# Float32 residual by accumulating transposes, and two moved steps in an attention and convolution kernel

## The chip, the cores and the metric

The kernel runs on one core of a Trainium2 chip. A core has five engines that work side by side, each with its own queue in program order: TensorE (PE, matrix products, written to PSUM), VectorE (DVE), ScalarE (ACT), GpSimd (POOL) and SyncE (SP), which here issues all transfers. They wait for each other through semaphores only. The metric is the device time of one execution in microseconds.

## What is computed

Cut to what matters. `x` is (4, 1024, 1024) float32, `cond` (4, 1024); 16 heads of 64.

```python
scale, shift = split(cond[:, None] @ W_emb + b_emb)
xn = rms_norm(x, g_norm) * (1.0 + scale) + shift
q, k, v = heads(xn @ W_qkv)                # (b, 16, n, 64) each
q, k = rms_norm(q, g_q), rms_norm(k, g_k)
attn = softmax(q @ k.T * d ** (-0.5))
o = merge(attn @ v)
x = x + (o + o @ W_out)
y = depthwise_causal_conv1d(x, cond)       # 4 taps per channel
return x + (y + b)
```

## The kernel before, in words

**Units and pairs.** The main part is `U = 32` units, four batches of eight; a unit `u` is one pair of heads of one batch. Within a unit run eight pairs `p`, 0 to 7; each takes 128 query rows of both heads against all 1024 keys. The units are unrolled, and for each engine the order of work within a pair is written out by hand in a function `unit`. A float32 operand is carried as a high and a low float16 part, and a product is made of three float16 ones.

**The softmax chain of a pair.** `score` (L946, 12 matmuls) writes both heads' logits; DVE takes each head's maximum (L1531) and makes the bias from it (L1534); ACT takes the exponential with that bias (L1187) and the high half (L1195); DVE takes the low half (L1540). `score` of the next pair writes over the same PSUM, so it waits for both exponentials (`exp_done`). The halves are transposed by DMA and go into `attend` (L965); `inverses` (L978) are two float32 transposes of the reciprocal sums, read by ACT (L1255).

**Beside it on TensorE.** `project` (L1002) makes q, k and v of the next unit in pairs 0 to 4; `stacks` (L1014) transposes them into key and query stacks. `stacks` of the second half in pair 7 writes the keys to `misc` and then the queries to `proj[:, 0]`.

**The output.** From unit 8 on (`outs`), a unit also makes output block `T = u - 8`, 512 channels (on the partitions, 128 at a time) of 256 positions, in four products `out_product(T, par, hh, i)`, one for each 128 channels: 24 float16 matmuls with `W_out` (L1036), then two float32 matmuls that add the transposed block of x (L1042). The identity operand `eye_x` of these holds the factor `back = 1 / y_scale`, since PSUM holds the output in another scale; DVE sets the two scales of the batch in `y_now` (`set_scale`) and ACT scales the identity (`scaled_eye`), every second unit. Products (0,0) and (0,1) go to bank `proj[:, 0]`, (1,0) and (1,1) to `proj[:, 1]`. `read_y(T, hh)` on ACT (L1286) copies one bank to `yT`, times `y_scale`; `convolve` on DVE (L1673 to L1684) makes the taps of a quarter of it; `out_transposes` (L1054, four float32 transposes) and `read_out` (L1299) turn it back, and SP stores it.

**Where they stood.** On TensorE, products (0,0) and (0,1) in pair 5, (1,0) in pair 6, (1,1) in pair 7. `read_y(T, .., 0)` on ACT stood at the head of pair 6, `read_y(T, .., 1)` in pair 0 of the next unit. The query stacks of pair 7 wait for `y_ev` of that first read, as they write over its bank:

```python
stacks(w, 1, 1, misc[:], (h_ev, 3 * w + 1))
stacks(w, 1, 0, proj[:, 0, :], (y_ev, 2 * T + 1) if outs else ...
```

**The end.** Unit 31 has no next unit; block 23 is made in its pairs 0 to 3, and 24 begun in pairs 4 to 7 (`tail_begin`, and `add_x`, L1023, for its residual). The blocks 25 to 31 follow one after another (`tail_product`), with their x in nine buffers `last_xr` that SP fills late. A product of block T there is followed by transposes of block T-1 or T-2. POOL's list has the powers (L1447), low halves (L1452, L1461, L1472, L1476) and nothing of the output.

## Time and profile before

| | us |
|---|---|
| median of 3 runs | 2456.92 (2450.82 to 2458.89) |
| the profiled execution, its own time | 2456.85 |
| its span, first to last instruction | 2454.9 |
| TensorE (PE) busy | 2337.2, 95% |
| DVE busy | 2061.2, 84% |
| ACT busy | 1797.1, 73% |
| POOL busy | 648.6, 26% |
| L1036, products with W_out, 3072 matmuls | 273 ns each |
| L1042 and L1023, residual, 512 records | 275 ns each |
| granted TensorE clock, mean | 0.992 |

How to read it: a matmul's length in the records includes a pipeline that overlaps the next one; what one costs in a stream is the distance from start to start. A float32 matmul stands in the trace as two records, a float32 transpose as one. TensorE being busy for 95% doesn't tell by itself whether it sets the end, since another engine may finish each step at the same moment; for that one needs the order of time around the waits.

### The profile page before, as it was taken

The numbers are of one execution on the slowest core, as the hardware profiler recorded it, in microseconds if no ns is written. First come the engines' busy times: TensorE is split into PE (matmuls) and PEld (weight loads), VectorE is DVE, ScalarE is ACT, GpSimd is POOL, SyncE is SP. The second block draws the span as 40 slices with busy tenths as digits, with TensorE's granted clock in tenths as the row PEclk, the third lists the DMA queues.
The fourth block names the chain that finished last, engine by engine and source line by source line (L and its number), as shares of the span: only waits on it lengthen the run. The fifth ranks groups of instructions, "written<-read, shape, count | busy, mean of one in ns | idle before, by whom it ended". The sixth has DMA issues, their size and how long they took to land.

```text
span 2454.9 us, 53605 instructions
## 1 busy us (share of the span) xinstructions
PE 2337.2 (95%) x20666; PEld 1529.3 (62%) x20666; DVE 2061.2 (84%) x3239; ACT 1797.1 (73%) x2706; POOL 648.6 (26%) x451
## 2 busy tenths in 40 slices
PE   5799898988899999999999999999999999999899
PEld 0455555555466666666666666666666666666688
DVE  7768988888878898888888888888888888888876
ACT  5467788788777777777777787777777777777732
POOL 1122333333333222323322223233212222222100
PEclk9899999999999999999999999999999999999999
DMA  8989989899999999999999999999988998889971
GB/s 361 315 208 230 194 177 200 180 189 225 202 207 181 203 183 215 182 200 231 204 208 191 213 183 201 192 189 222 208 177 172 182 175 162 177 162 176 186 187 52
DMA packets 1234732, 484.94 MB, mean 198 GB/s; under 512 B 1139632, under 2 KB 1197872, under 8 KB 1232048
## 3 DMA queue, kind: packets, MB, share of 16 engines
q1 hardware_dynamic: 1234480, 481.53, 93.4%
q8 instruction: 164, 2.69, 0.5%
q14 instruction: 88, 0.72, 0.1%
HBM read 137.20 MB, written 56.66 MB: 79 GB/s over the span
## 4 chain that ended last, share of the span: by engine, by line
PE 72%; DVE 11%; SPq 4%; issue 3%; ACT 2%; DMA 2%; POOL 1%; ACTq 0%; POOLq 0%
PE proj L1002 32%; PE proj L1036 12%; PE scores L946 11%; PE values L965 11%; DVE p_pair L1540 4%; DVE neg L1531 4%; SPq L750 3%; PE proj L1042 2%; PE values L978 1%; ACT p_pair L1195 1%; DMA w_sb<-w_dram 1%; PE misc L1054 1%; PE misc L1014 1%; PE proj L1014 1%; SPq L706 1%
## 5 line engine op out<-in xcount | busy, mean ns | idle before, releaser
L1002 PE MATMUL proj<-w_sb,xn_sb 128*128 128x384 f16 x6144 | 1034.1, 327 | 26.4 <-DMA w_sb<-w_dram 18.2
L1002 PEld LDWEIGHTS proj<-w_sb,xn_sb 128*128 128x128 f16 x6144 | 592.8, 98 | 431.3 <-issue 50.4
L1187 ACT ACTIVATE late<-scores,bias,l_scale 128x1024 f32<-128x1024 f32 x512 | 615.9, 1204 | 332.6 <-DVE bias L1534 313.7
L1540 DVE TENSOR_TENSOR p_pair<-late,p_pair 128x1024 f16<-128x1024 f32 x512 | 616.4, 1245 | 173.5 <-ACT p_pair L1195 173.2
L1531 DVE TENSOR_REDUCE neg<-scores 128x1 f32<-128x1024 f32 x512 | 623.2, 1217 | 101.7 <-PE scores L946 98.7
L1195 ACT ACTIVATE p_pair<-late 128x1024 f16<-128x1024 f32 x512 | 510.0, 1046 | 0.0
L965 PE MATMUL values<-pT,v_pair 128*64 128x256 f16 x6144 | 385.3, 275 | 13.2 <-ACT inv_all L1255 13.2
L946 PE MATMUL scores<-late 64*128 64x512 f16 x3072 | 376.1, 378 | 18.1 <-ACT late L1187 17.6
L965 PEld LDWEIGHTS values<-pT,v_pair 128*64 128x64 f16 x6144 | 316.4, 110 | 91.8 <-issue 70.1
L1447 POOL TENSOR_TENSOR rs<-ms,power 128x16 f32<-128x16 f32 x63 | 183.1, 2906 | 400.2 <-DVE ms L1554 399.9
L1036 PE MATMUL proj<-late,wo 128*128 128x256 f16 x2304 | 267.5, 273 | 0.8 <-DMA late<-in_x 0.8
L1476 POOL TENSOR_TENSOR oT_pair<-oT,oT_pair 128x256 f16<-128x256 f32 x124 | 148.4, 1197 | 436.2 <-ACT oT_pair L1264 436.2
L946 PEld LDWEIGHTS scores<-late 64*128 64x128 f16 x3072 | 128.9, 94 | 197.8 <-issue 45.0
L1036 PEld LDWEIGHTS proj<-late,wo 128*128 128x128 f16 x2304 | 222.3, 98 | 30.4 <-issue 5.8
L1452 POOL TENSOR_TENSOR qk_pair<-stage,qk_pair 128x512 f16<-128x512 f32 x126 | 147.1, 1189 | 327.2 <-ACT qk_pair L1218 327.2
L1684 DVE SCALAR_TENSOR_TENSOR late<-late,taps 128x256 f32<-128x256 f32 x324 | 157.1, 485 | 11.6
L1255 ACT ACTIVATE inv_all<-values 128x256 f32<-128x256 f32 x128 | 48.9, 382 | 139.0 <-PE values L978 138.9
L1203 ACT ACTIVATE stage<-proj 128x384 f32<-128x384 f32 x256 | 123.0, 480 | 25.4 <-PE proj L1002 25.4
L1534 DVE TENSOR_SCALAR bias<-neg,l_scale 128x1 f32<-128x1 f32 x512 | 109.6, 214 | 18.1
L1472 POOL TENSOR_TENSOR pair<-x_in,pair 128x1024 f16<-128x1024 f32 x24 | 66.9, 2788 | 207.2 <-ACT pair L1249 199.7
L1187 ACT ACTIVATION_READ_ACCUMULATOR late<-scores,bias,l_scale 128x1 f32 x512 | 98.6, 193 | 0.0
L1036 PE MATMUL proj<-xn_sb,wo 128*128 128x256 f16 x744 | 86.5, 273 | 0.8 <-ACT late L1286 0.8
(178 smaller groups left out, 1939.2 us busy)
## 6 DMA issues: line engine op xcount, KB each, us to landing
w_sb<-w_dram SPq DMA_DIRECT2D x121, 384.0 KB, 4.1
o_dram<-oT_pair SPq DMA_DIRECT2D x124, 128.0 KB, 2.4
out<-late SPq DMA_DIRECT2D x54, 256.0 KB, 2.9
x_in<-in_x SPq DMA_DIRECT2D x25, 512.0 KB, 4.8
late<-in_x SPq DMA_DIRECT2D x25, 512.0 KB, 4.2
wq_raw<-in_L_cond_W_qkv SPq DMA_DIRECT2D x8, 1536.0 KB, 10.7
late<-o_dram SPq DMA_DIRECT2D x12, 1024.0 KB, 6.3
xn_dram<-late SPq DMA_DIRECT2D x21, 512.0 KB, 3.3
```

Of the source, the lines that this page charges most:

```text
L946: last = nc.tensor.matmul(scores[:, h, n * HN:(n + 1) * HN], stack[rows_, par, i, p * P:(p + 1) * P], stack[rows_, par, j, n * HN:(n + 1) ...
L965: last = nc.tensor.matmul(values[DH * h:DH * h + DH, 0:QG].rearrange("p (a n) -> p a n", a=2), v_pair[:, par, 2 * c + h, DH * i:DH * i + D ...
L1002: last = nc.tensor.matmul(proj[:, t % 2, 0:6 * DH], xn_sb[:, t, i * K + c, :], w_sb[:, c, j, :], start=(c == 0 and i == j == 0), stop=(c = ...
L1036: last = nc.tensor.matmul(dst, const["wo"][:, c, b, m * P:(m + 1) * P], oT_[:, c, a, :], start=(c == 0 and a == b == 0 and c1 == K), stop= ...
L1187: nc.scalar.activation(prob[:, h, :], scores[:, h, :], ACT.Exp, bias=bias[:, s:s + 1], scale=const["l_scale"][:, 0:1], accum_out=total[:, ...
L1195: nc.scalar.activation(p_pair[:, s % 4, 0, :], prob[:, h, :], ACT.Copy).then_inc(hi_done, 1)
L1447: nc.gpsimd.tensor_tensor(rs[:], ms[:], const["power"][:, 0:4 * KH], ALU.pow).then_inc(h_pw, 1)
L1452: last = nc.gpsimd.tensor_tensor(qk_pair[:, j, 1].rearrange("p t (h d) -> p (t h) d", d=DH), stage[:, hf, :, j * DH:(j + 1) * DH], qk_pair ...
L1476: nc.gpsimd.tensor_tensor(o_half(u, g, 1), oT[:], o_half(u, g, 0), ALU.subtract).then_inc(o_low, 1)
L1531: nc.vector.tensor_reduce(neg[:, s:s + 1], scores[:, h, :], axis=AX.X, op=ALU.max, negate=True).then_inc(max_done, 1)
L1540: nc.vector.tensor_tensor(p_pair[:, s % 4, 1, :], prob[:, h, :], p_pair[:, s % 4, 0, :], ALU.subtract).then_inc(lo_done, 1)
L1684: nc.vector.scalar_tensor_tensor(out=acc_[:, m, :], in0=y_[:, m, k:k + QG], scalar=const["taps"][:, k, c:c + 1], in1=acc_[:, m, :], op0=AL ...
```

## The change

The residual's two float32 matmuls of a product become two float32 transposes against the plain identity that accumulate onto the product in PSUM. The factor `back` goes into x itself: a new POOL operation `x_residual(T)` multiplies the loaded block (128x1024 float32) in place, in pair 3 of a unit, in pairs 0, 2 and 4 of unit 31, and behind it for the rest. TensorE waits for its semaphore `xr_up` where it waited for the load and the scaled identity. `eye_x`, `one`, `y_now`, `set_scale` and `scaled_eye` are gone; `read_y` takes its scale from `const["y_scale"]`. The second product of a unit moves from pair 5 to pair 6, the first read of the output on ACT from pair 6 to pair 7. The diff, without tiles, semaphores and calls that only lose an argument:

```diff
@@ -1016,13 +1012,12 @@
                 last.then_inc(h_tr, 1)
 
             def add_x(hh, xr_):
-                pe.wait_ge(last_xr_ld[1], 16)
-                pe.wait_ge(eye_done, U - K + 2)
+                pe.wait_ge(xr_up, U - K + 1)
                 for i in range(2):
                     for a in range(2):
                         nc.tensor.matmul(proj[:, hh, i * QG + a * P:i * QG + (a + 1) * P],
-                                         xr_[:, a, (2 * hh + i) * P:(2 * hh + i + 1) * P], eye_x[:],
-                                         start=False, stop=False)
+                                         xr_[:, a, (2 * hh + i) * P:(2 * hh + i + 1) * P], const["eye32"][:],
+                                         start=False, stop=False, is_transpose=True)
 
             def out_product(T, par, hh, i, oT_, xr_, free, c0=0, c1=K):
                 m = 4 * par + 2 * hh + i
@@ -1040,7 +1035,7 @@
                     return
                 for a in range(2 if c0 == 0 else 0):
                     last = nc.tensor.matmul(dst[:, a * P:(a + 1) * P], xr_[:, a, (2 * hh + i) * P:(2 * hh + i + 1) * P],
-                                            eye_x[:], start=False, stop=(a == 1))
+                                            const["eye32"][:], start=False, stop=(a == 1), is_transpose=True)
                 if i == 1:
                     last.then_inc(op_mm, 1)
                 elif T == U - 1 and hh == 1:
@@ -1068,8 +1063,7 @@
 
             def tail_product(i, hh, c0=0):
                 T, g = U - K + i, i // 2
-                free = ((last_oT_ld[g], 16), (o_low, NG * (U - 1) + g + 1), (last_xr_ld[i + 1], 16),
-                        (eye_done, U - K + 2), (y_ev, 2 * T + hh - 1))
+                free = ((last_oT_ld[g], 16), (o_low, NG * (U - 1) + g + 1), (xr_up, T + 1), (y_ev, 2 * T + hh - 1))
                 for m in range(2):
                     out_product(T, i % 2, hh, m, last_oT[g], last_xr[i + 1], free if m == 0 else (), c0)
 
@@ -1111,18 +1105,20 @@
                     if outs and p >= 5 and not last:
                         if T == 0 and p == 5:
                             pe.wait_ge(wo_lo, K)
-                        free0 = ((oT_ld, 8 * (T - par) + 16), (xr_ld, 16 * (T + 1)), (eye_done, T - par + 2),
+                        free0 = ((oT_ld, 8 * (T - par) + 16), (xr_up, T + 1),
                                  (qkv_ev, K * w + 7) if qkv else (y_ev, 2 * T - 1))
                         free1 = ((h_ev, 3 * w + 2) if qkv else (y_ev, 2 * T),)
                         if p == 5:
                             out_product(T, par, 0, 0, oT_in, xr, free0)
+                        elif p == 6:
                             out_product(T, par, 0, 1, oT_in, xr, ())
+                            out_product(T, par, 1, 0, oT_in, xr, free1)
                         else:
-                            out_product(T, par, 1, p - 6, oT_in, xr, free1)
+                            out_product(T, par, 1, 1, oT_in, xr, ())
                     if last and p < 4:
                         hh = p // 2
                         out_product(T, par, hh, p % 2, oT_in, last_xr[0],
-                                    ((oT_ld, 8 * (T - par) + 16), (last_xr_ld[0], 16), (eye_done, T - par + 2),
+                                    ((oT_ld, 8 * (T - par) + 16), (xr_up, T + 1),
                                      (y_ev, 2 * T) if hh else (h_ev, 3 * U)))
                     elif last:
                         tail_begin((p - 4) // 2, p % 2)
@@ -1269,14 +1265,7 @@
                 nc.scalar.activation(const["wo"][:, c, 0, :], wo_raw[c], ACT.Copy,
                                      scale=wo_top[:, 3:4]).then_inc(wo_hi, 1)
 
-            def scaled_eye(T):
-                act.wait_ge(y_set, T + 2)
-                need(act, op_mm, 2 * T)
-                nc.scalar.activation(eye_x[:], const["eye32"][:], ACT.Copy,
-                                     scale=y_now[:, 1:2]).then_inc(eye_done, 2)
-
-            def read_y(T, scales, hh):
-                act.wait_ge(y_set, scales)
+            def read_y(T, hh):
                 act.wait_ge(op_mm, 2 * T + hh + 1)
                 if T == U - K - 1:
                     act.wait_ge(h_lo, 2 * U)
@@ -1285,14 +1274,14 @@
                     need(act, cv, 16 * (T - (2 if static(T) and T >= U - K else 1)) + 8 * (hh + 1))
                 nc.scalar.activation(yT_of(T)[:, 2 * hh:2 * hh + 2, H:H + QG],
                                      proj[:, hh, :].rearrange("p (m n) -> p m n", m=2), ACT.Copy,
-                                     scale=y_now[:, 0:1]).then_inc(y_ev, 1)
+                                     scale=const["y_scale"][:, T:T + 1]).then_inc(y_ev, 1)
 
             def read_last_y(i):
                 T = U - 1
                 act.wait_ge(*((op_first, 1), (op_mm, 2 * U))[i])
                 act.wait_ge(cv, 16 * (T - 1))
                 nc.scalar.activation(yT_of(T)[:, 2 + i, H:H + QG], (proj[:, 1, 0:QG], last_y)[i], ACT.Copy,
-                                     scale=y_now[:, 0:1]).then_inc((y_first, y_ev)[i], 1)
+                                     scale=const["y_scale"][:, T:T + 1]).then_inc((y_first, y_ev)[i], 1)
 
             def read_out(T, hh):
                 act.wait_ge(f_tr, 2 * T + hh + 1)
@@ -1315,7 +1304,7 @@
                         if has_early(u):
                             read_projection(w, 1)
                         if fins:
-                            read_y(T - 1, T + par, 1)
+                            read_y(T - 1, 1)
                         if xs:
                             x_square(v, par, 2, x_in[:], (x_ld, 16 * (u + 1)), pair[:, 1], (xT_in, 16 * u))
                     if p in (1, 2, 3) and qkv and not has_early(u):
@@ -1326,9 +1315,9 @@
                             squares(w, 1, (h_ss, 2 * w + 1))
                         if fins:
                             read_out(T - 1, 1)
+                    if p == 7 and outs and not last:
+                        read_y(T, 0)
                     if p == 6:
-                        if outs and not last:
-                            read_y(T, T - par + 2, 0)
                         if qkv:
                             read_stacks(w, 1 - par, 0, 0, 0, misc[:])
                             read_stacks(w, 1 - par, 0, 1, 1, proj[:, 1, :])
@@ -1370,14 +1359,10 @@
                     if p == 4:
                         if qkv:
                             read_projection(w, 6)
-                        if outs and par == 0:
-                            scaled_eye(T)
                         if qkv:
                             high_halves(w, 0)
                     if p == 5 and qkv:
                         high_values(w, 1 - par, 1)
-                    if last and p == 5:
-                        scaled_eye(U - K)
 
             for v in range(K):
                 x_high(v, first_x[v], first_pair[v % 4], (xn_in[v - 4], 16) if v >= 4 else (x_mod, 0))
@@ -1475,10 +1459,20 @@
                 pool.wait_ge(o_hi, NG * u + g + 1)
                 nc.gpsimd.tensor_tensor(o_half(u, g, 1), oT[:], o_half(u, g, 0), ALU.subtract).then_inc(o_low, 1)
 
+            def x_residual(T):
+                i = T - (U - K - 1)
+                pool.wait_ge(*((xr_ld, 16 * (T + 1)) if i < 0 else (last_xr_ld[i], 16)))
+                block_ = xr[:] if i < 0 else last_xr[i]
+                nc.gpsimd.tensor_scalar(block_, block_, const["back"][:, T:T + 1], 1.0, ALU.mult,
+                                        ALU.mult).then_inc(xr_up, 1)
+
             def unit(u, par, qkv, xs, outs, fins):
-                w, v = u + 1, u + K
+                w, v, T = u + 1, u + K, u - K
                 begun = not (static(u) and u == 0)
+                last = u + 1 == U
                 for p in range(K):
+                    if last and p in (0, 2, 4):
+                        x_residual(T + p // 2)
                     if p == 0 and xs:
                         x_power(v, par, 2)
                     if p == 1 and begun:
@@ -1487,6 +1481,8 @@
                         x_low(v, x_in[:], pair)
                     if p == 3 and begun:
                         o_lower(u - 1, 3)
+                    if p == 3 and outs and not last:
+                        x_residual(T)
                     if p == 4 and qkv:
                         half_power(w, 0)
                         half_low(w, 0)
@@ -1519,8 +1515,12 @@
             low_values(0, 0, 0)
             low_values(0, 0, 1)
             in_units(unit, pool)
-            for g in range(2, 4):
-                o_lower(U - 1, g)
+            o_lower(U - 1, 2)
+            for T in range(U - K + 2, U - K + 4):
+                x_residual(T)
+            o_lower(U - 1, 3)
+            for T in range(U - K + 4, U):
+                x_residual(T)
 
         @block.vector
         def _(dve):
@@ -1650,13 +1650,6 @@
                 dve.wait_ge(pv_done, n + 1)
                 need(dve, o_low, n)
                 nc.vector.tensor_tensor(oT[:], values[:, 0:QG], inv_all[:], ALU.mult).then_inc(o_done, 1)
-
-            def set_scale(T):
-                need(dve, y_ev, 2 * T)
-                need(dve, eye_done, T)
-                for i, name in enumerate(("y_scale", "back")):
-                    nc.vector.tensor_scalar(y_now[:, i:i + 1], one[:], const[name][:, bass.ds(T, 1)], None,
-                                            ALU.mult).then_inc(y_set, 1)
 
             def convolve(T, par, hh, i):
                 n = 4 * T + 2 * hh + i
@@ -1705,8 +1698,6 @@
                     if p in (2, 4, 6):
                         invert(u, p // 2 - 1, par)
                     if p == 2:
-                        if outs and par == 0:
-                            set_scale(T)
                         if fins:
                             convolve(T - 1, 1 - par, 1, 0)
                     if p == 3 and fins:
```

On TensorE, from the inverses of pair 5 on in a unit with an output block (`proj<-late,wo` is a product with W_out, `proj<-eye_x,late` its residual, `misc<-eye,qk_pair` and `proj<-eye,qk_pair` stacks). Before:

```order
L978 MATMUL values<-eye,inv_wide 128x128 x2
L1036 MATMUL proj<-late,wo 128x256 x24
L1042 MATMUL proj<-eye_x,late 128x128 x2
L1036 MATMUL proj<-late,wo 128x256 x24
L1042 MATMUL proj<-eye_x,late 128x128 x2
L1014 MATMUL misc<-eye,qk_pair 128x128 x8
L1014 MATMUL proj<-eye,qk_pair 128x128 x8
L965 MATMUL values<-pT,v_pair 64x256 x24
L946 MATMUL scores<-late 128x512 x12
L965 MATMUL values<-pT,v_pair 64x256 x24
L1036 MATMUL proj<-late,wo 128x256 x24
L1042 MATMUL proj<-eye_x,late 128x128 x2
```

And now:

```order
L974 MATMUL values<-eye,inv_wide 128x128 x2
L1031 MATMUL proj<-late,wo 128x256 x24
L1037 MATMUL proj<-eye,late 128x128 x2
L1010 MATMUL misc<-eye,qk_pair 128x128 x8
L1010 MATMUL proj<-eye,qk_pair 128x128 x8
L961 MATMUL values<-pT,v_pair 64x256 x24
L942 MATMUL scores<-late 128x512 x12
L961 MATMUL values<-pT,v_pair 64x256 x24
L1031 MATMUL proj<-late,wo 128x256 x24
L1037 MATMUL proj<-eye,late 128x128 x2
L1031 MATMUL proj<-late,wo 128x256 x24
L1037 MATMUL proj<-eye,late 128x128 x2
```

The second product stands behind the scores and the attention product of pair 6, directly ahead of the third.

On ACT, from the value halves of pair 5 to the exponentials of pair 7 (`inv_all<-values` is the read of the inverses that opens pair 7). Before:

```order
L1226 ACTIVATE v_pair<-stage 128x8x64
L1286 ACTIVATE late<-proj,y_now 128x2x256
L1231 ACTIVATE late<-misc 128x2x512
L1231 ACTIVATE late<-proj 128x2x512
L1218 ACTIVATE qk_pair<-stage 128x512 x2
L1187 ACTIVATE late,total<-scores,bias,l_scale 128x1024 x2
L1195 ACTIVATE p_pair<-late 128x1024 x2
L1264 ACTIVATE oT_pair<-oT 128x256
L1255 ACTIVATE inv_all<-values 128x256
L1231 ACTIVATE late<-misc 128x2x512
```

And now:

```order
L1222 ACTIVATE v_pair<-stage 128x8x64
L1227 ACTIVATE late<-misc 128x2x512
L1227 ACTIVATE late<-proj 128x2x512
L1214 ACTIVATE qk_pair<-stage 128x512 x2
L1183 ACTIVATE late,total<-scores,bias,l_scale 128x1024 x2
L1191 ACTIVATE p_pair<-late 128x1024 x2
L1260 ACTIVATE oT_pair<-oT 128x256
L1251 ACTIVATE inv_all<-values 128x256
L1275 ACTIVATE late<-proj,y_scale 128x2x256
L1227 ACTIVATE late<-misc 128x2x512
```

The read `late<-proj` with the output's scale, ahead of both stack reads of pair 6 before, stands between the read of the inverses and that of the key stacks in pair 7.

On POOL, from the low halves of the attention output in pairs 7, 1 and 3 (`oT_pair`, x3) to that of pair 5 (`rs<-ms,power` is the power of pair 4). Before, in the last unit but one:

```order
L1476 TENSOR_TENSOR oT_pair<-oT,oT_pair 128x256 x3
L1447 TENSOR_TENSOR rs<-ms,power 128x16
L1452 TENSOR_TENSOR qk_pair<-stage,qk_pair 128x512 x2
L1461 TENSOR_TENSOR v_pair<-stage,v_pair 128x8x64
L1476 TENSOR_TENSOR oT_pair<-oT,oT_pair 128x256
```

And now:

```order
L1460 TENSOR_TENSOR oT_pair<-oT,oT_pair 128x256 x3
L1466 TENSOR_SCALAR late<-late,back 128x1024
L1431 TENSOR_TENSOR rs<-ms,power 128x16
L1436 TENSOR_TENSOR qk_pair<-stage,qk_pair 128x512 x2
L1445 TENSOR_TENSOR v_pair<-stage,v_pair 128x8x64
L1460 TENSOR_TENSOR oT_pair<-oT,oT_pair 128x256
```

The scaling of x (`late<-late,back`) stands behind the low half of pair 3 and ahead of the power.

## Rows read from the trace of the kernel before

**Rows 1.** Unit 17: us, busy (instructions) of PE, PEld, DVE, ACT, POOL, then clock.
```profile
1300.20:1370.90 70.70, 70.70 (x642) 47.14 (x640) 61.46 (x96) 54.84 (x84) 21.00 (x14) 1.00 0.93 189
```

**Rows 2.** Order of time on ACT, pairs 5 to 7: start us, length us, instruction, [idle before].
```profile
1346.58 0.38 ACT L1255 ACTIVATE inv_all<-values 128x256 f32<-128x256 f32 x1 [1.80 <-PE values L978]
1346.86 0.48 ACT L1203 ACTIVATE stage<-proj 128x384 f32<-128x384 f32 x1
...
1359.33 1.20 ACT L1187 ACTIVATE late<-scores,bias,l_scale 128x1024 f32<-128x1024 f32 x1
...
1362.82 0.38 ACT L1255 ACTIVATE inv_all<-values 128x256 f32<-128x256 f32 x1
1363.26 1.02 ACT L1231 ACTIVATE late<-misc 128x1024 f16<-128x1024 f16 x1
1365.39 1.20 ACT L1187 ACTIVATE late<-scores,bias,l_scale 128x1024 f32<-128x1024 f32 x1 [1.10 <-DVE bias L1534]
...
1366.77 1.20 ACT L1187 ACTIVATE late<-scores,bias,l_scale 128x1024 f32<-128x1024 f32 x1
```

**Rows 3.** Order of time on TensorE, the same stretch.
```profile
1349.45 2.78 PE L1036 MATMUL proj<-late,wo 128*128 128x256 f16 x24
1352.07 0.61 PE L1042 MATMUL proj<-eye_x,late 128*128 128x128 f32 x4
1352.52 0.61 PE L1014 MATMUL misc<-eye,qk_pair 128*128 128x128 f16 x8
...
1354.94 1.47 PE L946 MATMUL scores<-late 64*128 64x512 f16 x12
...
1360.94 1.47 PE L946 MATMUL scores<-late 64*128 64x512 f16 x12
...
1363.06 0.61 PE L1014 MATMUL proj<-eye,qk_pair 128*128 128x128 f16 x8
...
1368.12 1.47 PE L946 MATMUL scores<-late 64*128 64x512 f16 x12
```

**Rows 4.** Order of time in the last unit: TensorE, ACT and DVE.
```profile
2291.56 2.78 PE L1036 MATMUL proj<-late,wo 128*128 128x256 f16 x24 [0.77 <-DMA late<-in_x]
...
2293.97 1.21 ACT L1187 ACTIVATE late<-scores,bias,l_scale 128x1024 f32<-128x1024 f32 x1
...
2295.32 1.47 PE L946 MATMUL scores<-late 64*128 64x512 f16 x12 [0.53 <-ACT late L1187]
...
2298.52 1.22 DVE L1531 TENSOR_REDUCE neg<-scores 128x1 f32<-128x1024 f32 x1
```

**Rows 5.** Order of time on DVE, pairs 6 and 7 of unit 17.
```profile
1356.44 1.23 DVE L1531 TENSOR_REDUCE neg<-scores 128x1 f32<-128x1024 f32 x1
...
1363.88 1.22 DVE L1531 TENSOR_REDUCE neg<-scores 128x1 f32<-128x1024 f32 x1
```

**Rows 6.** Order of time on TensorE in the tail, float32 transposes.
```profile
2393.84 0.60 PE L1054 MATMUL misc<-eye,late 128*128 128x128 f32 x4
2394.28 2.78 PE L1036 MATMUL proj<-xn_sb,wo 128*128 128x256 f16 x24
```

**Rows 7.** POOL: line 1472 over the span (ns min/median/max), and unit 17 in time.
```profile
L1472 POOL TENSOR_TENSOR pair<-x_in,pair x24: 2128/3084/3091, 155.6 to 1741.1; 128x1024 f16<-128x1024 f32 x24
...
1336.94 2.91 POOL L1447 TENSOR_TENSOR rs<-ms,power 128x16 f32<-128x16 f32 x1 [11.41 <-DVE ms L1554]
```

**Rows 8.** Order of time in the tail, DVE and then TensorE.
```profile
2352.86 1.95 DVE L1684 SCALAR_TENSOR_TENSOR stage<-stage,taps 128x256 f32<-128x256 f32 x3
...
2355.38 1.52 DVE L1684 SCALAR_TENSOR_TENSOR stage<-stage,taps 128x256 f32<-128x256 f32 x3
...
2376.32 0.23 DVE L1673 TENSOR_SCALAR stage<-ends,carry 128x3 f32<-128x3 f32 x1 [6.52 <-issue]
...
2440.81 0.23 DVE L1673 TENSOR_SCALAR stage<-ends,carry 128x3 f32<-128x3 f32 x1 [2.29 <-ACT stage L1286]
...
2380.65 0.66 PE L1054 MATMUL misc<-eye,stage 128*128 128x128 f32 x4
```

More of the change, by code:

```diff
@@ L1417, in _ @@
             in_units(unit, act)
[L1418 to L1420 removed]
+            read_y(U - K, 0)
+            read_y(U - K, 1)
             o_high(U - 1, 2)
[L1422 removed]
+            read_y(U - K + 1, 0)
             read_inverses(U - 1, 3)
             read_out(U - K - 1, 0)
[L1425 removed]
+            read_y(U - K + 1, 1)
             read_out(U - K - 1, 1)
@@ L1429, in _ @@
             for T in range(U - K + 2, U):
-                read_y(T, scales, 0)
+                read_y(T, 0)
                 read_out(T - 2, 1)
                 if T + 1 < U:
-                    read_y(T, scales, 1)
+                    read_y(T, 1)
                 else:
@@ L1719, in unit @@
                         normalise(w, 1)
-                    if last and p == 5:
-                        set_scale(U - K)
                     if u in (1, 2) and p < 4:
@@ L1745, in unit @@
                         normalise(w, 1)
-            nc.vector.memset(ends[:], 0.0)
-            nc.vector.memset(one[:], 1.0).then_inc(one_done, 1)
-            dve.wait_ge(one_done, 1)
+            nc.vector.memset(ends[:], 0.0).then_inc(ends_set, 1)
+            dve.wait_ge(ends_set, 1)
             for v in range(K):
```

17 lines of the change are left out of this document (4 added, 13 removed).

## The prediction

> **What bounds the kernel now.** I read the granted clock and busy shares first, then one steady unit window by window, then TensorE's, ACT's and DVE's instructions of pairs 5 to 7 in order of time, then the tail. The profiled execution took 2456.85 us (its span is 2454.9), the median of the three runs is 2456.92, so the sum is made against 2456.85 and needs no shift.
>
> Unit 17 is typical of units 9 to 30: score group to score group it takes 70.7 us, and TensorE is busy in all of it at a clock of 1.00 [rows 1]. That invites the short answer, that whatever is taken from TensorE comes off the time. The second view corrects it. In [rows 2] ACT's second exponential of pair 7 starts at 1366.77 and lasts 1.20, so it ends at 1367.97; the next unit's score group in [rows 3] starts at 1368.12, 0.15 us later. Where a score group is shown waiting for an exponential, the distance is the same: 2293.97 + 1.21 to 2295.32, 0.14 [rows 4]. So at the end of each unit TensorE and the softmax chain arrive **together**. The same distance at pair 7 is 1360.94 - (1359.33 + 1.20) = 0.41, so there the slack is 0.26 us. Two paths of equal length lead from pair 5 to the next unit: TensorE's own work, and ACT and DVE.
>
> What sets the second path: ACT's exponentials of pair 5 and their high halves, DVE's low halves and normalisation, then DVE's maximum of pair 6 at 1356.44 with no wait for scores [rows 5]; then the exponentials of pair 6, their high halves, DVE's maximum of pair 7 at 1363.88, again with no wait for scores, and the exponential at 1365.39 that waits for DVE's bias [rows 2, 5]. Nothing in it waits for TensorE after the inverses of pair 5, for which ACT waited 1.80 us at 1346.58.
>
> **Part 1, the residual's cost on TensorE.** Each output product ends in two float32 multiplications of a 128x128 block of x by the scaled identity. The trace has them as four records that take 1352.52 - 1352.07 = 0.45 us on TensorE [rows 3], 0.225 us each. Float32 transposes by the same identity exist in the kernel: four of them take 2394.28 - 2393.84 = 0.44 us [rows 6], 0.11 us each. No transpose here accumulates; I take the plain one's price because the moved columns are the same, with the multiplication's 0.225 as the upper bound. So a product gets shorter by 2 x 0.115, about 0.225 us, and a unit's four by 0.9 us. The Trainium skill (TensorE: Matmul & The Clock Gate, Terms) says that transpose mode is 4x faster for FP32; the trace shows about 2x between these two forms. By the page a transpose would cost 0.056 us, each product would save another 0.11 us, and the sum below would end near 2463 us.
>
> **Part 2, the second product moves from pair 5 to pair 6.** Before, it was 1352.07 - 1349.45 = 2.62 us and its residual 0.45 [rows 3]. Pair 6's scores, at 1354.94, now come those 3.07 and another 0.225 of the first product earlier, at 1351.64. DVE doesn't take them up before 1356.44, busy with low halves and normalisation [rows 5]. From pair 6's scores to pair 7's it was 1360.94 - 1354.94 = 6.00 us; it becomes 6.00 - 0.225 + 2.62 + 0.225 = 8.62, so TensorE is back at 1360.26 and pair 7's scores wait for the exponential: 1360.53 + 0.15 = 1360.68 instead of 1360.94. Of 0.68 us that TensorE had saved by then, 0.26 is left. (If pair 6's scores had to wait for the exponential of pair 5, 0.4 us of that would be free.) The other waits of the moved product are older: the bank of the third product is read by ACT ahead of the pair-6 exponentials, over 2 us before TensorE gets there.
>
> **Part 3, ACT's first read of the output moves from pair 6 to pair 7.** Before, it ran ahead of the pair-6 exponentials, long before TensorE wrote the query stacks over the same bank at 1363.06. Now it stands in ACT's queue behind the read of the inverses of pair 7. That read starts at 1362.82 [rows 2] and is fixed by the pair-6 exponentials and high halves, not by TensorE. A following ACT instruction starts 0.28 us after such a read (1346.58, 1346.86), so the output read starts at 1363.10; 0.69 long, it ends at 1363.79, and with 0.15 us to TensorE the stacks can start at **1363.94**. TensorE, back 0.26 us earlier than before, at 1362.80, waits some 1.1 us. Behind that wait on TensorE are the query stacks, the fourth product, the attention product and the next unit's scores: 1368.12 - 1363.06 = 5.06 before, 4.83 with the cheaper residual. The next unit's scores start at 1363.94 + 4.83 = 1368.77, against 1368.12. So a unit grows by **0.65 us**. Bounds: 0.55 if the release takes only 0.05 us, 0.75 if ACT's queue needs another 0.1.
>
> What is late next: ACT's read of the key stacks, 1.02 us at 1363.26 before, follows the output read and ends by 1364.8, before the bias that lets the exponential go at 1365.39, so the softmax chain keeps its times. In pairs 0 to 4 of the next unit TensorE is the bound (busy throughout [rows 1]), so the lateness is carried to pair 5, where ACT starts from TensorE's inverses again. It adds up from unit 9 to unit 30: 22 x 0.65 = **+14.3 us**.
>
> **Part 4, POOL's scaling of x.** A new POOL operation on 128x1024 float32 with one input, 32 times. The nearest row is POOL's two-input operation of that size, 2.1 to 3.1 us [rows 7]; with one input for two, half of the shortest, 1.1 us, is the lower bound, and I take 2. In a steady unit it stands before the power at 1336.94, ahead of which POOL was idle for 11.4 us [rows 7]; x is needed in pair 5, some 10 us after that. It is hidden at any of these prices. The Trainium skill (GPSIMD Engine Reference, 4.1 and 8) calls one-input work on GPSIMD roughly line-rate, and warns that it shares its SBUF interfaces with VectorE, a rule against the change. The trace shows such contention in the tail [rows 8], priced there. In the steady unit it falls into pair 3, where the softmax chain has slack.
>
> In unit 31 the first product already waits for x: it starts at 2291.56 after 0.77 us for the DMA [rows 4]. POOL's scaling comes on top, 1.1 to 3.1 us. Pair 1's scores, at 2295.32, would start up to 2.3 us later, but DVE takes them up only at 2298.52 [rows 4], 3.2 us after their start; I take **+0.2**, with 0 to 0.5 as bounds. Unit 31's pairs are set by the exponentials, so TensorE's savings there bring nothing, and its first scores' lateness of 0.65 is absorbed.
>
> In the tail TensorE is the bound only from 2380.65: there its transposes needed the first two convolutions that DVE had begun at 2376.32, after 6.52 us of idling while stores had to land [rows 8]. From there to the product behind which DVE's last four convolutions begin at 2440.81 stand 18 products: 18 x 0.225 = **-4.05**. Six scalings on POOL run next to DVE's convolutions, of which three steps took 1.95 instead of 1.52 us next to one short operation on POOL [rows 8]. Only those after 2376 count: **+0.5**, bounds 0 and 1.5.
>
> **Part 5, what is removed.** DVE's tiny scales and ACT's scaled identities stand in pairs 2 and 4, where TensorE is the bound: nothing.
>
> **Sum.** 14.3 + 0.2 - 4.05 + 0.5 = +10.95, so 2456.85 + 10.95 = **2467.8 us**. With the bounds, 12.1 to 16.5, 0 to 0.5, -4.05, 0 to 1.5: 2464.9 to 2471.3.
>
> **Rivals.**
> - *The read is in time.* If ACT gets to its output read about 0.65 us earlier than I place it, scores of the next unit stay tied to the exponential, with neither gain nor loss in a unit. Then only the tail counts: -4.05 + 0.7, 2453.5 us. For it: ACT still idled 1.10 us before the exponential [rows 2]. Against: that idle time lies behind the read, not before it.
> - *TensorE's saving arrives in full.* If the softmax chain can follow, each of 23 units gets 0.9 us shorter and the tail 4.05: 2432 us. This is the faster side; it decides where the exponential of pair 7 ends 0.9 us earlier. For it: TensorE is busy throughout. Against: the 0.15 us, and DVE's maxima that wait for no scores.
> - *An accumulating float32 transpose costs what the multiplication does.* Then the stacks' wait is not softened: 0.88 per unit, 22 x 0.88 = 19.4, nothing in the tail, +0.7: 2477 us. Nothing in the trace shows the accumulating form.
> - *The change doesn't do what it says:* excluded by the order of instructions, which shows both moves.
>
> **How the numbers follow.** Forecast 0.60, read in time 0.17, full saving 0.10, costly transposes or more contention 0.13. A measurement tells about 0.3%, 7.4 us, from no change. Slower by more: 0.9 of the forecast and all of the last case, 0.67. Faster by more: the full saving and a little, 0.11. The rest, 0.22, is within. The range takes in the read in time and the upper bounds, 2451 to 2474, and leaves out the full saving and most of the costly case.
>
> **What would show it.** After: a unit of 71.3 to 71.4 us instead of 70.7; two idle stretches on TensorE per unit, some 0.4 us before pair 7's scores and about 1.1 us before the query stacks, ended by ACT's output read; the next unit's scores 0.8 us after the exponential's end instead of 0.15; the residual's two records at 0.22 us together; in the tail, two products and four transposes together 0.45 us shorter. Wrong would be a unit at or under 70.7 us, no wait before the stacks, or POOL's scaling over 3.1 us.

## The result, and the profile after

The changed kernel takes 2464.41 us in the median of 11 runs (2458.64 to 2471.34), the kernel before 2458.19 in 11 runs beside them (2450.82 to 2467.18). The ratio is 1.003, with a 95% interval of 1.0015 to 1.0044: slower by 0.3%, some 7.4 us. The forecast was +10.95 us, just above the interval's upper end (3.7 to 10.8 us). The sign and the mechanism were right; the measured change is a third smaller than the forecast.

TensorE's busy time fell from 2337.2 to 2313.6 us, and the kernel got slower. From the page of the kernel after:

```profile
span 2456.8 us, 53026 instructions
...
PE 2313.6 (94%) x20410; PEld 1500.5 (61%) x20410; DVE 2062.1 (84%) x3212; ACT 1787.2 (73%) x2693; POOL 701.9 (29%) x483
```

The profiled execution took 2458.64 us, only 1.8 more than the profiled one of before. Its steady units began 4.5 us earlier (the score group of unit 8 at 657.3 instead of 661.8), and units 0 to 7 hold none of the changed steps; that start differs as much among the eleven other builds of this study, from 657.4 to 663.7. So the two traces are compared by stretches behind it: per unit, in unit 31, and in the tail.

Order of time on TensorE, pairs 5 to 7 of unit 17, kernel after (start us, length us, instruction, [idle before <- what ended it]); it answers to [rows 3]:

```profile
1343.73 1.47 PE L942 MATMUL scores<-late 64*128 64x512 f16 x12
...
1350.66 1.47 PE L942 MATMUL scores<-late 64*128 64x512 f16 x12
...
1353.49 2.79 PE L1031 MATMUL proj<-late,wo 128*128 128x256 f16 x24
1356.12 0.38 PE L1037 MATMUL proj<-eye,late 128*128 128x128 f32 x2
1356.34 2.78 PE L1031 MATMUL proj<-late,wo 128*128 128x256 f16 x24
...
1359.66 1.47 PE L942 MATMUL scores<-late 64*128 64x512 f16 x12 [0.32 <-ACT late L1183]
1361.06 0.44 PE L974 MATMUL values<-eye,inv_wide 128*128 128x128 f32 x2
...
1362.80 0.61 PE L1010 MATMUL proj<-eye,qk_pair 128*128 128x128 f16 x8 [0.85 <-ACT late L1275]
...
1367.61 1.47 PE L942 MATMUL scores<-late 64*128 64x512 f16 x12
```

The residual's two transposes take 1356.34 - 1356.12 = 0.22 us. Both forecast idle stretches are there: 0.32 us ahead of pair 7's scores, 0.85 us ahead of the query stacks, ended by ACT's output read. The order of time on ACT, same stretch, which answers to [rows 2]:

```profile
1358.31 1.20 ACT L1183 ACTIVATE late<-scores,bias,l_scale 128x1024 f32<-128x1024 f32 x1
...
1361.40 0.41 ACT L1260 ACTIVATE oT_pair<-oT 128x256 f16<-128x256 f32 x1
1361.70 0.37 ACT L1251 ACTIVATE inv_all<-values 128x256 f32<-128x256 f32 x1
1361.97 0.69 ACT L1275 ACTIVATE late<-proj,y_scale 128x512 f32<-128x512 f32 x1
1362.54 1.03 ACT L1227 ACTIVATE late<-misc 128x1024 f16<-128x1024 f16 x1
1364.37 1.20 ACT L1183 ACTIVATE late<-scores,bias,l_scale 128x1024 f32<-128x1024 f32 x1 [0.80 <-DVE bias L1534]
...
1365.74 1.20 ACT L1183 ACTIVATE late<-scores,bias,l_scale 128x1024 f32<-128x1024 f32 x1
```

The last exponential ends at 1366.94 and the next unit's scores start at 1367.61, 0.67 us later (0.8 was forecast); before it was 0.15. So ACT and DVE are no longer what holds them, but the wait in front of the stacks. From pair 5's scores to the end of that exponential it is 23.21 us, before 23.26: the softmax chain kept its times.

### The profile page after: what moved, and what is told of

The parts are those of the page before. It is cut to its first block, busy times and chain, and to the rows that moved or that the text cites. A ratio compares the mean times of both kernels' runs of the same rounds, so it can differ in the third digit from the quotient of the medians.

```text
span 2456.8 us, 53026 instructions
## 1 busy us (share of the span) xinstructions
PE 2313.6 (94%) x20410; PEld 1500.5 (61%) x20410; DVE 2062.1 (84%) x3212; ACT 1787.2 (73%) x2693; POOL 701.9 (29%) x483
## 4 chain that ended last, share of the span: by engine, by line
PE 57%; DVE 19%; issue 8%; ACT 7%; SPq 4%; DMA 2%; POOL 1%; ACTq 0%; POOLq 0%; DVEq 0%
PE proj L998 31%; PE scores L942 9%; PE values L961 9%; DVE p_pair L1540 6%; DVE neg L1531 6%; PE proj L1031 5%; ACT p_pair L1191 3%; SPq L746 2%; ACT late L1183 1%; DVE stage L1562 1%; DVE bias L1534 1%; PE values L974 1%; PE misc L1049 1%; DMA w_sb<-w_dram 1%; SPq L702 1%
## 5 line engine op out<-in xcount | busy, mean ns | idle before, releaser
L1214 ACT ACTIVATE qk_pair<-stage 128x512 f16<-128x512 f32 x126 | 72.0, 621 | 22.9 <-DVE stage L1566 22.9
## 6 DMA issues: line engine op xcount, KB each, us to landing
wq_raw<-in_L_cond_W_qkv SPq DMA_DIRECT2D x8, 1536.0 KB, 10.3
```

## The experiments

Ratios are to the kernel before on the same chip, with 95% intervals. "Unit" is the distance from score group to score group in unit 17; the three numbers behind it are pairs 5, 6 and 7. Before: 70.70 (10.23, 6.01, 7.17). After: 71.17 (6.93, 9.00, 7.95).

### The transposes without the moves, and the moves without the transposes

`e1_transposes_only` is the kernel after with both moved steps put back:

```diff
                         if p == 5:
                             out_product(T, par, 0, 0, oT_in, xr, free0)
-                        elif p == 6:
                             out_product(T, par, 0, 1, oT_in, xr, ())
-                            out_product(T, par, 1, 0, oT_in, xr, free1)
                         else:
-                            out_product(T, par, 1, 1, oT_in, xr, ())
+                            out_product(T, par, 1, p - 6, oT_in, xr, free1)
```

with ACT's `read_y(T, 0)` again at the head of pair 6. `e2_moves_only` makes the same two moves in the kernel before.

> The changed kernel with both moves taken back: the second product again in pair 5, ACT's first read of the output again in pair 6; the accumulating transposes and POOL's scaling stay. Theory (at the end of a unit TensorE and the softmax chain were equally long before, so TensorE's shorter work brings nothing in a unit): a steady unit stays at 70.7 us, the next unit's scores 0.15 us after the exponential, TensorE idle about 0.9 us more per unit in pairs 6 and 7; only the tail gains about 4 us, unit 31 loses about 1.3: ratio to before 0.999, some 2454 us. Rival (TensorE's saving arrives in full once the read is not in its way): a unit of 69.8 us, ratio 0.990, some 2434 us.

> The kernel before with the two moves alone: float32 multiplications by the scaled identity stay, nothing is added to POOL. Theory (the moved read of the output makes the query stacks wait, and the dearer residual behind it isn't softened): the unit grows by the 0.47 us that the change showed plus 0.22 for one product's residual, 70.7 to 71.4; 22 units give 15 us, no gain in the tail: ratio 1.006. Rival (the loss of the change comes from POOL's scaling and its contention with DVE): a unit of 70.7 us, ratio 1.000.

e1: 0.9987 (0.9977 to 0.9997), unit 70.66 (9.77, 6.17, 7.43). e2: 1.0077 (1.0061 to 1.0093), unit 71.54 (7.16, 9.07, 8.02). TensorE of e1 at the end of the unit:

```profile
1362.48 1.47 PE L942 MATMUL scores<-late 64*128 64x512 f16 x12 [0.32 <-ACT late L1181]
...
1369.91 1.25 PE L942 MATMUL scores<-late 64*128 64x512 f16 x10 [0.43 <-ACT late L1181]
```

The two waits for exponentials, 0.32 and 0.43 us, hold most of the 0.9 that four cheaper residuals saved; a unit gains 0.04. This speaks against "TensorE's saving arrives in full". The moves alone cost 0.84 us a unit, near the 0.88 that the prediction gave for moves with the dear residual, and the transposes soften that to 0.47. As e2 has nothing new on POOL, the loss belongs to the moves and not to POOL's scaling.

### The wait taken away in two ways

`e3_queries_last` keeps both moves, but TensorE does the fourth product ahead of the query stacks, so that it has work while ACT reads:

```diff
                         stacks(w, 1, 1, misc[:], (h_ev, 3 * w + 1))
-                        stacks(w, 1, 0, proj[:, 0, :], (y_ev, 2 * T + 1) if outs else ...
...
                             out_product(T, par, 1, 1, oT_in, xr, ())
+                            stacks(w, 1, 0, proj[:, 0, :], (y_ev, 2 * T + 1))
```

`e10_read_end_of_six` moves ACT's `read_y(T, 0)` ahead of the high half of the attention output, out of the queue behind the inverses' read.

> The changed kernel with the fourth product on TensorE put ahead of the query stacks in pair 7, so that the stacks come some 2.9 us later, long after ACT's read of the output. Theory (the wait for that read is the whole loss in a unit, and behind it stands the exponential): the wait of 0.85 us before the stacks is gone, the unit falls from 71.17 to 70.7 us and not below, since the scores of the next unit are again 0.15 us after the exponential; with the tail's gain some 2454 us, ratio 0.998. Rival (the wait was only one symptom and the TensorE path is the bound): a unit of 70.2 us or less, ratio below 0.994.

> The changed kernel with ACT's first read of the output one place earlier: at the end of pair 6, between the high halves and the high half of the attention output, so ahead of the read of the inverses and no longer behind TensorE's inverses of pair 7. Theory (the wait comes from the read's place behind the read of the inverses): TensorE's wait before the query stacks shrinks from 0.85 to 0.3 us or less, the next unit's scores are again 0.15 to 0.2 us after the exponential, the unit is 70.7 us, ratio 0.998 to 0.9995. Rival (any place of the read after pair 6's exponentials costs the same, or the delayed inverses make the attention product late): 71.2 us, ratio 1.003.

e3: 0.9998 (0.9985 to 1.0011), unit 70.67 (6.93, 9.01, 7.44). e10: 0.9979 (0.9965 to 0.9993), unit 70.66 (6.93, 9.00, 7.43). TensorE of e10, where the stacks still wait, but too shortly to matter:

```profile
1363.19 0.61 PE L1010 MATMUL proj<-eye,qk_pair 128*128 128x128 f16 x8 [0.28 <-ACT late L1275]
```

In both, the next scores follow the exponential by 0.15 us again, and pair 7 is 7.43 or 7.44 long, as in e1. That is the state of the rival "the read is in time": a unit is tied to the exponential and has neither gain nor loss, and the rival's -3.35 us lies within e10's interval. So the wait before the stacks is shown to be all of a unit's loss. e3, e10 and e1 have the same unit and ratios of 0.9998, 0.9979 and 0.9987 with intervals that overlap. In their traces pair 0 of unit 31 takes 12.53, 12.02 and 10.70 us; as e10 has the lowest ratio, that doesn't explain their order, which stays open.

### The other path made shorter

If the second path is as long as the first, shortening it is what turns TensorE's saving into time. In pair 5 ACT reads the last projection and squares it behind the read of the inverses, for which it waits 1.80 us [rows 2]. "Early squares" puts that work in front, into the wait:

```diff
+                    if p == 5 and qkv and outs:
+                        read_projection(w, 7)
+                        squares(w, 1, (h_ss, 2 * w + 1))
                     if p % 2 == 1 and p >= 3:
                         read_inverses(u, (p - 3) // 2)
...
                     if p == 5:
-                        if qkv:
+                        if qkv and not outs:
                             read_projection(w, 7)
```

It was put into the kernel before (e5), e1 (e6), e3 (e7) and the kernel after (e8).

> The kernel before with one thing changed on ACT: in units with an output block, the last read of the projection and the squares stand ahead of the read of the inverses in pair 5, in time that ACT idled away (1.80 us), instead of behind it, so the softmax chain of pairs 5 to 7 starts about 1.1 us earlier. Theory (two paths of equal length): TensorE's own work still takes 70.65 to 70.7 us a unit, so nothing is gained, ratio 1.000; only the distance from exponential to next scores grows from 0.15 to about 1.2 us. Rival (the softmax chain alone sets the unit and TensorE is only along with it): a unit of 69.6 us, ratio 0.990.

> The accumulating transposes and POOL's scaling without the two moves, and with ACT's squares ahead of the inverses in pair 5. Theory (each of the two changes alone brings nothing, as the other path is as long; together both paths get shorter): a unit falls from 70.7 by TensorE's 0.9 us to about 69.8 us, 23 units give 20 us and the tail 4: ratio 0.991, some 2433 us. Rival (another wait takes over, such as DVE's maxima or the normalisation that waits for POOL's power): a unit above 70.2 us, ratio over 0.995.

> The changed kernel with the fourth product ahead of the query stacks and with ACT's squares ahead of the inverses in pair 5. Theory: the wait for ACT's read is gone, the softmax chain is 1.1 us shorter, so TensorE's own 69.8 us are the bound again: ratio 0.991. If the two moves of the change are of use by themselves, they must show here as a unit below that of the kernel with the transposes and the early squares alone; by the theory both have 69.8 us. Rival: with pair 7's scores still behind the exponential (slack gone there by 0.3 us) a unit of 70.1 us or more, and the moves are a loss.

> The changed kernel with only ACT's squares ahead of the inverses in pair 5; the query stacks stay where they are and wait for ACT's read in pair 7. Theory (the wait is measured from the softmax chain, which starts 1.1 us earlier): the read comes 1.1 us earlier, TensorE arrives at the stacks about 0.85 us before it now, so nearly all of the wait goes, the unit falls from 71.17 to 70.1 us at most and perhaps to 69.8: ratio to before 0.994 or less. Rival (the read is tied to TensorE's inverses of pair 7): the unit stays above 70.7 us.

| | ratio | unit (pairs 5, 6, 7) |
|---|---|---|
| e5, before | 0.9995 (0.9986 to 1.0003) | 70.71 (10.23, 6.01, 7.16) |
| e6, transposes only | 0.9956 (0.9942 to 0.9969) | 70.24 (9.77, 5.78, 7.39) |
| e7, transposes, moves, queries last | 0.991 (0.9896 to 0.9924) | 69.77 (6.93, 8.62, 6.93) |
| e8, the change as it is | 0.9987 (0.9975 to 0.9999) | 70.62 (6.93, 8.62, 7.79) |

The expectation for e5 failed in its second half: the distance at the unit's end did not grow. That for e6 failed too, as it wanted the unit that e7 has, and so did that for e8, which wanted 70.1 us at most. DVE's first maximum of pair 6 tells why, in e5, e6 and e7 in this order, one line from each:

```profile
1351.77 1.22 DVE L1534 TENSOR_REDUCE neg<-scores 128x1 f32<-128x1024 f32 x1 [0.84 <-PE scores L946]
```

```profile
1349.72 1.23 DVE L1532 TENSOR_REDUCE neg<-scores 128x1 f32<-128x1024 f32 x1 [0.39 <-PE scores L942]
```

```profile
1350.15 1.22 DVE L1535 TENSOR_REDUCE neg<-scores 128x1 f32<-128x1024 f32 x1
```

There is a third tie. In the kernel before, pair 6's scores come 10.23 us after pair 5's, and with a shorter softmax chain (e5) DVE stands 0.84 us waiting for them. Its maximum then starts 1.50 us after the scores' start (1350.27 in e5), as soon as they are there. In the kernel before it is also 1.50 us, 1354.94 to 1356.44 [rows 3, 5], though no wait is shown. The cheaper residuals of pair 5 bring them 0.46 us earlier, and that is what e6 gains (70.70 - 70.24 = 0.46). Only with one product fewer ahead of them, at 6.93, do they stop counting, and e7 gets 0.93 us a unit. So the move on TensorE is of use once the chain is shorter, and costs a unit nothing until then (e3). It was not run apart from the read in pair 7 and the later query stacks, in which e7 differs from e6 too; that the gain is its own rests on the three lines above. What takes that back is ACT's read in pair 7 together with query stacks that wait for it at their old place: e8 differs from e7 only in where the query stacks stand, and its TensorE and ACT show

```profile
1360.45 0.44 PE L974 MATMUL values<-eye,inv_wide 128*128 128x128 f32 x2
...
1362.03 0.61 PE L1010 MATMUL proj<-eye,qk_pair 128*128 128x128 f16 x8 [0.70 <-ACT late L1275]
```

```profile
1360.92 0.38 ACT L1251 ACTIVATE inv_all<-values 128x256 f32<-128x256 f32 x1 [0.24 <-PE values L974]
1361.20 0.68 ACT L1275 ACTIVATE late<-proj,y_scale 128x512 f32<-128x512 f32 x1
```

ACT now has time to spare and waits 0.24 us for TensorE's own inverses, yet the stacks wait 0.70 us: the output read is queued behind the read of the inverses that TensorE makes directly ahead of the stacks. The shorter chain on ACT doesn't mend that; another order did (e7). Whether e10's order, with the read at the end of pair 6, would do as well together with the early squares was not run. Over 22 units the 0.85 us between e8 and e7 is 18.7 us, and their medians differ by 18.75 (2454.33 and 2435.58, the same chip). That the two agree so closely is in part chance, since in the traces e7's unit 31 takes 3.45 us longer than e8's (55.69 and 52.24).

### POOL's scaling, and the last unit's load

`e11_scaling_twice` (a single run) has a second multiplication, by 1.0, behind each scaling of x. `e4_early_load` issues the load of unit 31's x in pair 2 of unit 30 instead of pair 7.

> The changed kernel with POOL's scaling done twice, the second time by 1. Theory (POOL's scaling is hidden in a steady unit, by 9.35 us of idling ahead of the power): the unit stays at 71.17 us to the hundredth, and only unit 31 and the tail grow, by 1 to 3 us. Rival (contention with DVE costs in the steady unit): the unit grows by 0.1 us or more.

> The changed kernel with the load of x for the last unit's first product issued in pair 2 of unit 30 instead of pair 7. Theory (in unit 31 TensorE waited 2.91 us for load and scaling together, and the product after it ran at a granted clock of 0.66, 4.3 instead of 2.6 us): the wait and the slow clock both go, pair 0 of unit 31 falls from 10.4 to about 7.5 us, the pairs after it are paced by the exponentials, so 1.3 to 3 us in all: ratio 0.999 to the change, 1.002 to before. Rival (the slow clock there has another cause): the product still takes 4.3 us.

e11: 2470.35 us, unit 71.17, the same as after. One scaling more in every unit costs nothing there: POOL's price in the steady units is hidden, as forecast. In unit 31 pair 0 is 12.80 us instead of 10.40, and the tail, from pair 7's scores of unit 31 to the end, is 114.43 instead of 109.76. TensorE waits there for DVE, and DVE is slowed. Three of its convolution steps in e11's tail next to scalings, and three of the same form once POOL is done:

```profile
2390.89 3.78 DVE L1681 SCALAR_TENSOR_TENSOR stage<-stage,taps 128x256 f32<-128x256 f32 x3
...
2396.94 1.53 DVE L1681 SCALAR_TENSOR_TENSOR stage<-stage,taps 128x256 f32<-128x256 f32 x3
```

Of the 4.67 us that the tail grew, 4.55 lie ahead of the transposes that wait for these steps (at 2398.53, 44.56 us after pair 7's scores; after has them at 40.01). So the expectation was right on the unit and too low on the rest: unit 31 and the tail grew by 7.1 us, not by 1 to 3.

e4: 1.0027 (1.0015 to 1.0038), unit 71.17. Pair 0 of unit 31 is 6.96 us instead of 10.40, but pair 1 is 8.78 instead of 7.09, pair 2 7.41 instead of 6.09 and the tail 110.98 instead of 109.76; of 3.4 us won nothing arrives that the ratio could tell. Pair 1 takes 1.69 us back because DVE isn't ready for its scores until 3.20 us after their start (2307.26 and 2304.06), as in the kernel before. Why pair 2 and the tail got longer stays open.

### All three together

`e9_all_three` is e7 with the early load.

> The change with the fourth product ahead of the query stacks, ACT's squares ahead of the inverses in pair 5, and the early load for unit 31. Theory: a unit of 69.8 us as without the early load, and pair 0 of unit 31 at 7 to 7.5 us instead of 11.9, of which the pairs behind it, paced by the exponentials, keep 1 to 3 us: ratio 0.990. Rival (the tail is set by transfers and gives it back, as the early load alone brought 0.03% only): ratio 0.991, the same as without it.

It takes 2431.69 us in the median of 4 runs, ratio 0.9893 (0.9876 to 0.991), and beats both kernels. TensorE is again busy in all of a unit, at 1.00, and the unit is shorter; the row answers to [rows 1]:

```profile
1287.30:1357.07 69.77, 69.77 (x634) 46.19 (x632) 61.54 (x96) 54.97 (x84) 23.04 (x15) 1.00 0.98 191
```

Against the kernel before, the stretch from unit 8's scores to unit 31's is 20.5 us shorter (1605.56 and 1626.07), unit 31 is as long, and the tail gives 109.87 - 114.06 = -4.2, together -24.7 us; the ratio is -26.3, with an interval of -22.1 to -30.5. The early load makes unit 31 2.7 us shorter than in e7's trace (52.95 and 55.69), but its own share of the ratio, 1.7 thousandths, is within the intervals.

## Why the prediction was right, and where its size was off

**Two paths of equal length: right.** The short answer from TensorE's 95% would have been 2432 us. e1 shows it wrong by nearly all of it. What the prediction missed is the third tie, between pair 6's scores and DVE's maxima. It took "with no wait for scores" [rows 5] as a sign that these scores were early; e5 shows that DVE and TensorE came together there too, and the 1.50 us from the scores' start to the maximum, the same in e5 and in the kernel before, is the sign that could have been read. It didn't touch the sum, since the change moved these scores away.

**The residual's price: right.** 0.22 us for two accumulating transposes against 0.45, so they cost what the plain ones do [rows 6]. The Trainium skill's 4x (TensorE: Matmul & The Clock Gate, Terms) isn't what start to start distances show here; they show 2x.

**The wait before the stacks: right in kind, 0.65 us mis-sized, 0.47 measured.** The step that was off is "that read starts at 1362.82 and is fixed by the pair-6 exponentials and high halves, not by TensorE". After, the read of the inverses starts 0.30 us behind the instruction ahead of it (1361.40, 1361.70); before it was 0.40. From the kernel before, on TensorE and then on ACT:

```profile
1362.34 0.44 PE L978 MATMUL values<-eye,inv_wide 128*128 128x128 f32 x2
...
1362.42 0.41 ACT L1264 ACTIVATE oT_pair<-oT 128x256 f16<-128x256 f32 x1
```

TensorE's inverses stood at 1362.34, and where ACT is seen waiting for them the read follows 0.47 us after their start (e8: 1360.45 and 1360.92). 1362.34 + 0.47 is 1362.81: before, it was TensorE that held it, by the 0.1 us between 0.30 and 0.40. No wait is shown at that place, so this rests on the two distances. With pair 7's scores 0.30 us earlier against pair 5's this fell away. Against pair 5's scores the read came 0.14 us earlier than placed, the output read with it, and the stacks at 19.07 us instead of 19.23. The rest of the step held: 0.69 for the read, 0.83 from its start to the stacks (0.84 forecast), 4.81 from there to the scores (4.83). Over 22 units the term is 10.3 us and not 14.3. From unit 8's scores to unit 31's this pair of traces has only 9.45 (1626.07 and 1635.52), as two units of the kernel before were longer than the rest, in their pair 0: unit 15 with 70.87 and unit 23 with 71.42 us. The bounds, 0.55 to 0.75, had covered only the release and the queue, not the start of the read.

**Unit 31: +0.2 forecast, +1.29 measured.** Pair 0 is 10.40 us instead of 7.43, which is 2.97 more, and pair 1 7.09 instead of 8.78, which takes 1.69 back. The prediction added 2.3 us at most and found 3.2 of cover. Both were off. TensorE, POOL and DVE of the kernel after, answering to [rows 4]:

```profile
2294.19 1.50 PE L961 MATMUL values<-pT,v_pair 128*64 128x256 f16 x24
2298.60 4.45 PE L1031 MATMUL proj<-late,wo 128*128 128x256 f16 x24 [2.91 <-issue]
2302.88 0.38 PE L1037 MATMUL proj<-eye,late 128*128 128x128 f32 x2
```

```profile
2297.38 1.12 POOL L1466 TENSOR_SCALAR late<-late,back 128x1024 f32<-128x1024 f32 x1 [8.72 <-DMA late<-in_x]
```

```profile
2304.70 1.23 DVE L1531 TENSOR_REDUCE neg<-scores 128x1 f32<-128x1024 f32 x1 [1.67 <-PE scores L942]
```

POOL took 1.12 us, the lower bound. But x landed later, so that POOL began 4.59 us after the unit's scores, where TensorE could begin 3.67 us after them before, and the product behind the wait took 2302.88 - 2298.60 = 4.28 us instead of 2.62. This stretch's row (after the busy times comes the granted clock):

```profile
2298.00:2303.00 5.00, 4.40 (x26) 3.36 (x26) 3.37 (x7) 3.80 (x7) 1.53 (x2) 0.66 1.06 245
```

The clock was 0.66 on the mean, so for a part of it TensorE ran at 1.2 GHz, after it had idled 2.91 us. Neither the later landing nor the slower clock was in the sum.

The cover was counted from the wrong end. DVE can take up scores only once they are made: its maximum starts 1.51 us after pair 1's scores (2303.19, 2304.70). The 3.2 us of before [rows 4] were measured from their start, so the cover was 3.20 - 1.51 = 1.69 us, and 2.97 - 1.69 = 1.28 us go through. It is the same slip as with pair 6's scores above.

**The tail: -4.05 + 0.5 forecast, -4.3 measured.** From pair 7's scores of unit 31 to the end it is 109.76 us instead of 114.06. The point from which TensorE is the bound, the transposes at 2380.65 [rows 8], comes at 2387.03, 40.01 us after those scores instead of 39.82. So up to there POOL's scalings and the cheaper residuals nearly cancel. The contention can be seen, in TensorE and then in DVE:

```profile
2373.06 0.66 PE L1049 MATMUL misc<-eye,late 128*128 128x128 f32 x4 [1.71 <-DVE late L1677]
```

```profile
2370.69 2.32 DVE L1677 SCALAR_TENSOR_TENSOR late<-late,taps 128x256 f32<-128x256 f32 x3
...
2381.79 0.25 DVE L1666 TENSOR_SCALAR stage<-ends,carry 128x3 f32<-128x3 f32 x1 [4.26 <-ACT late L1275]
2381.94 1.31 DVE L1670 TENSOR_SCALAR stage<-stage,taps,conv_b 128x256 f32<-128x256 f32 x1
```

Three steps take 2.32 us next to a scaling and 1.53 elsewhere, the step at 2381.94 1.31 instead of 0.41; but most of it falls into time that was idle. The +0.5 measured +0.19. From 2387.03 to DVE's last four convolutions, at 2443.03, it is 56.00 us instead of 2440.81 - 2380.65 = 60.16, which is -4.16 for the forecast -4.05; the rest to the end gives 0.3 more. In the steady part, two products and four transposes:

```profile
2393.20 0.60 PE L1049 MATMUL misc<-eye,stage 128*128 128x128 f32 x4
...
2399.32 0.60 PE L1049 MATMUL misc<-eye,late 128*128 128x128 f32 x4
```

6.12 us, against 2400.41 - 2393.84 = 6.57 before: the 0.45 forecast.

**Sum by the traces:** 9.45 + 1.29 - 4.3 = +6.4 us, within the ratio's interval of 3.7 to 10.8. Against the forecast that is 4.85 us less in the units (4.0 by the step above, 0.9 by the two longer units of before), 1.09 more in unit 31 and 0.75 less in the tail. The errors have both signs, so the total is nearer than the terms.

## What to carry to other kernels

Look for the distance between the two candidates for the bound at every place where they meet, not only at the one where the waits end last: here an engine that is 95% busy was freed of 1% of its work and a unit gained 0.04 us (e1), and "it doesn't wait" doesn't say by how much: compare the start with the earliest one that its input allows. A read that frees a bank belongs in front of work that depends on the engine which will need that bank; behind it, it made a wait that a shorter chain on ACT didn't remove (e8). And a saving on one path is worth a try together with the shortening of the other: here 0.9987 and 0.9995 alone, 0.9956 together, 0.991 with the order that the two allow.

## What the runs showed of the hardware

**The clock after an idle stretch.** The same first product of unit 31, 24 matmuls, by how long TensorE had idled before it (the clock is the granted one over the product):

| | idle before, us | product, us | clock |
|---|---|---|---|
| e2, before, e8 | 0.39, 0.77, 2.43 | 2.62 each | 1.00 |
| after | 2.91 | 4.28 | 0.60 |
| e10 | 3.53 | 5.08 | 0.50 |
| e1 | 3.55 | 3.93 | 0.65 |
| e3 | 4.08 | 5.08 | 0.50 |
| e6 | 4.12 | 4.29 | 0.60 |
| e11 | 4.31 | 5.07 | 0.50 |
| e7 | 4.38 | 4.29 | 0.60 |

So in these traces a wait of 2.91 to 4.38 us cost 1.3 to 2.5 us more than its own length, and a longer wait did not always cost more. The row of e3 has the whole product at 1.2 GHz:

```profile
2295.00:2300.20 5.20, 5.14 (x25) 3.64 (x26) 2.80 (x4) 2.69 (x5) 1.59 (x1) 0.50 1.03 237
```

**POOL beside DVE.** POOL's scaling of 128x1024 float32 takes 1.12 us beside DVE's maxima (2297.38) and 2.08 where it starts beside DVE's low halves with their two inputs (in unit 17 they overlap for 1.10 us of it). Over the execution, the 25 of them on this tile:

```profile
L1466 POOL TENSOR_SCALAR late<-late,back x25: 1117/2082/2087, 685.6 to 2382.0; 128x1024 f32<-128x1024 f32 x25
```

In that place DVE's two low halves took 2.82 us before and 2.83 after, so the scaling cost DVE nothing and POOL paid alone. In the tail of e11 it was the other way round: three steps of DVE took 3.78 instead of 1.53 us, and POOL's beside them stayed at 1.04 to 1.28. The Trainium skill (GPSIMD Engine Reference, 4.1) calls one-input work there roughly line-rate; that agrees with the 1.12, and not with the 2.08.
